# A graph-attention kernel whose last layer multiplies its edge features over 128 rows of the array in place of 30

## What is computed

```python
h = (x @ W.T).reshape(n, H, D)                                # H = 8, D = 32
alpha = einsum('ehd,hd->eh', h[src], a_src) + einsum('ehd,hd->eh', h[dst], a_dst)
enc = relu(edge_attr @ edge_W.T + edge_b).reshape(-1, H, D)   # edge_attr: 53125 x 3
alpha = alpha + sum(enc * h[dst], axis=-1)
alpha = where(alpha >= 0, alpha, 0.2 * alpha)
attn = segment_softmax(alpha, dst)
out = segment_sum(h[src] * attn[..., None], dst) + bias
```

## Time and profile before

| | |
|---|---|
| time, median of 3 runs | 2092.96 us (2092.95 to 2096.61) |
| profiled execution, its own time | 2100.78 us |
| its span, first to last instruction | 2099.0 us |
| mean granted TensorE clock | 0.824 |
| PE busy | 1673.1 us (80%) |
| DVE busy | 1574.9 us (75%) |
| POOL busy | 1504.7 us (72%) |
| ACT busy | 1370.3 us (65%) |

### The profile page before, as it was taken

How to read it: one execution, slowest core, us unless ns; L and a number is a source line. 1 busy time by engine, 2 the same in 40 slices (tenths; PEclk the granted TensorE clock), 3 DMA queues, 4 the chain that set the end, 5 groups by cost and what they waited for, 6 DMA issues and landing times. The chain is left out here.

```text
span 2099.0 us, 43225 instructions
## 1 busy us (share of the span) xinstructions
PE 1673.1 (80%) x9241; PEld 1064.7 (51%) x9241; DVE 1574.9 (75%) x4409; ACT 1370.3 (65%) x5004; POOL 1504.7 (72%) x1648
## 2 busy tenths in 40 slices
PE   7377778777876577878878877789999999999984
PEld 5244445545544344545545444445565655565652
DVE  5567877777778456666656667879899998899997
ACT  3267776777675444545545446668888888888886
POOL 3677777777767577777777773667777777777873
PEclk9578877888787767777777787779999999999995
DMA  7655554555641344444444641434444444444431
GB/s 195 173 161 143 145 143 139 142 144 167 186 116 37 118 129 135 134 129 135 137 129 134 197 121 39 122 109 125 125 129 130 127 130 127 125 128 133 137 90 61
DMA packets 130636, 274.39 MB, mean 131 GB/s; under 512 B 39701, under 2 KB 65274, under 8 KB 130367
## 3 DMA queue, kind: packets, MB, share of 16 engines
q0 software_dynamic: 64128, 181.33, 32.1%
q1 hardware_dynamic: 61564, 86.45, 13.5%
q10 hardware_dynamic: 4699, 3.86, 0.7%
HBM read 255.00 MB, written 17.20 MB: 130 GB/s over the span
## 5 line engine op out<-in xcount | busy, mean ns | idle before, releaser
L1283 POOL DMA_INDIRECT rows<-table,index_all x1100 | 1073.7, 976 | 402.9 <-issue 304.9
L1801 PE MATMUL bank<-rows,onehot 128*128 128x264 f32 (+1 forms) x2200 | 863.2, 492 | 55.0 <-DVE rows L843 17.4
L854 DVE TENSOR_TENSOR sums<-sums,bank 128x264 f32 (+1 forms) x1320 | 556.8, 422 | 325.6 <-PE bank L1801 252.5
L1498 ACT ACTIVATE rows<-rows,wgt 128x33 f32<-128x33 f32 (+2 forms) x2740 | 706.3, 338 | 2.1 <-issue 1.1
L1801 PEld LDWEIGHTS bank<-rows,onehot 128*128 128x128 f32 x2200 | 416.7, 230 | 126.1 <-issue 77.7
L1721 PE MATMUL bank<-identb,onehotT 128*128 128x128 bf16 x1320 | 228.9, 261 | 41.9 <-issue 28.9
L1283 POOL DMA_INDIRECT late<-table,index_all x220 | 214.1, 973 | 67.0 <-issue 62.2
L1721 PEld LDWEIGHTS bank<-identb,onehotT 128*128 128x128 bf16 x1320 | 135.1, 117 | 155.0 <-issue 93.6
L1506 ACT ACTIVATE prod<-bank 128x512 f32<-128x512 f32 x240 | 134.1, 559 | 107.2 <-PE bank L1813 97.0
L1820 PE MATMUL bank<-late,onehotT 128*128 x1320 | 201.0, 290 | 1.3 <-DVE prod L863 1.3
L1450 ACT CAST onehot<-bank 128x768 f32<-128x768 bf16 x240 | 174.5, 729 | 40.5 <-PE bank L1721 40.3
(11 more groups left out here) (215 smaller groups left out, 2242.2 us busy)
## 6 DMA issues: line engine op xcount, KB each, us to landing
locb<-loc_d SPq DMA_DIRECT2D x120, 352.0 KB, 3.8
rows<-table,index_all POOLq DMA_INDIRECT x1100
flags<-flags_d SPq DMA_DIRECT2D x508, 27.5 KB
late<-table,index_all POOLq DMA_INDIRECT x220
table<-rows SPq DMA_DIRECT2D x25, 136.0 KB, 1.8
table<-rows SPq DMA_DIRECT2D x25, 134.0 KB, 2.7
late<-table SPq DMA_DIRECT2D x1, 3300.0 KB
table<-rows SPq DMA_DIRECT2D x25, 129.5 KB, 2.3
```

Source lines behind the costliest of these rows:

```text
L854: done(v.tensor_tensor(a, a, sum_bank(l, t, s)[:, 0:VV], ALU.add), "add")
L1283: g.indirect_dma_start(out=rows_of(l, t)[:, s, 0:ROW[l]], out_offset=None, in_=table[l], in_offset=bass.IndirectOffsetOnAxis(ap=index_all[ ...
L1498: i = a.activation(r, r, ACT.Copy, scale=wgt[:, t.u, h * B + s:h * B + s + 1])
L1801: done(m.matmul(sum_bank(l, t, s)[:, 0:VV], onehot[:, t.u, s, :], rows_of(l, t)[:, s, 0:VV], start=True, stop=True), "agg")
```

## The change

`attrT` is a view of all 128 rows in place of 30, so that the memset of L1264 sets 128 rows to one, and L1813 takes all 128 as its contraction. `edgew3` has 128 rows; a new DVE memset at the start of the program sets them to zero, before the DMAs that write rows 0 to 29. So rows 30 to 127 multiply ones by zeros. Sizes of what is read per row, DMAs and their bytes, and all waits stay.

```diff
-        edgew3 = sb("edgew3", [30, D], BF16)
+        edgew3 = sb("edgew3", [P, D], BF16)
...
-        attrT = lateb[0:30, BLOCKS * 3 * D:].rearrange("p (r f) -> p r f", r=RING)
+        attrT = lateb[:, BLOCKS * 3 * D:].rearrange("p (r f) -> p r f", r=RING)
...
             ones_cols(0)
             mark("ONES_DONE")
+            ch(v.memset(edgew3[:, :], 0.0))
```

## The result

The changed kernel takes 2077.41 us (median of 5 runs, 2071.16 to 2081.35) against 2092.96 us (2090.33 to 2096.61): 0.992 of before, 95% interval 0.9895 to 0.9945. That is faster by 15.6 us where 27.0 were forecast; the time lies inside the range, nearer its upper end. Its profiled execution took 2071.16 us, 29.6 us less than the profiled one of before.

What follows compares the result with a forecast made beforehand. PE was taken to bound low-clock periods, POOL full-clock ones at 16.3 us. From the profiled 2100.78 us, 22.8 (clock) and 3.6 (start) came off: 2074.4 us, or 2066 us on the timed scale, 7.8 us lower; range 2056 to 2082 us.

Steps and rivals of the forecast that it cites:

- The gaps on PE: On PE around each 30-row L1813: going from 128 rows and back costs 0.10 us each way, 0.20 us an encode, removed.
- POOL as the floor of a period: Last layer's full-clock periods: POOL's gathers and four scalings fill 16.3 us, so POOL sets their length.
- full-clock periods gain next to nothing: Last layer's periods at clock 1.00: a faster PE shows next to nothing, since POOL sets them.
- PE is the bound in low periods and gives back 1.2 us in each: Last layer's periods partly at 1.2 GHz: PE saves 0.20 us x 6, so 17.74 us becomes 16.5 us.
- The second case of the rivals: Clock falls as often, only the array's emptying goes: 18 us from the periods, 3.6 us from the start, 2071 us; chance 0.23.
- The clock: the likeliest case: Last layer's 35 periods: the clock stops falling and the low level's 22.8 us come back in full; chance 0.62.
- The start: Last layer's first two periods, bound by PE: 18 encodes x 0.20 us save 3.6 us, between nothing and 7 us.
- The sum: Whole kernel: profiled 2100.78 us less 22.8 and 3.6 gives 2074.4 us, or 2066 us on the timed runs' scale.
- No change: L1813's weight load still waits 0.20 us for the product before it; every period stays, 2093 us; chance 0.08.
- Slower, by more falls: Last layer: PE spends its saving waiting for POOL and DVE, the clock falls twice each period, 2124 us; chance 0.07.
- Memsets at no cost: POOL's L1264 memset takes 3.61 us whatever its rows, far bound 11.8 us more; DVE's 0.1 us falls ahead of an HBM wait.

## Why the prediction came out as it did

**The gaps on PE: right.** 0.60 to 0.50 and 0.32 to 0.22 us, and the weight load beside the sum. The cause needs a correction in size: the gaps stand at 30, 33 and 64 rows, and 65 are enough to avoid them.

**POOL as the floor of a period: wrong.** The sum of POOL's rows came out at 16.3 us, the period's length, and I took the equality for a proof. The earlier trace rows spoke against it: 1.3 us of the idle time that I counted as POOL's own are waits for PE, in five full-clock periods. DVE's 15.5 us looked like room, but its remaining 0.8 us were nothing that a faster PE took away: the full-clock period of the changed kernel has the same 16.30 us with DVE busy for 15.47. Leaving out POOL's work changed nothing; adding 0.39 us to DVE's made the period 0.33 us longer. The forecast that full-clock periods gain next to nothing came true by luck, since another engine sets about the same length. The number was right, the engine was not, and so the advice that follows from it would have been wrong as well: it is DVE's work that is worth moving.

**PE is the bound in low periods and gives back 1.2 us in each: mis-sized.** It measured 0.35 us (17.8 with 64 rows against 17.4 with 65 or 128). The low stretch of a period is short. In one of the kernel before, cut at the ends of its low stretch,

```profile
1553.39:1559.89 6.50, 6.33 (x46) 4.13 (x45) 5.96 (x16) 5.28 (x22) 5.62 (x8) 1.00 0.28 76
1559.89:1563.30 3.41, 3.41 (x14) 2.07 (x13) 3.24 (x9) 2.29 (x10) 2.60 (x3) 0.51 0.46 116
1563.30:1571.15 7.85, 7.15 (x48) 4.45 (x46) 6.69 (x16) 6.76 (x26) 4.93 (x6) 1.00 0.60 174
```

DVE is busy for 3.24 of 3.41 us even there, and the last 7.85 us run at 1.00 again. I read this so: PE's delay holds the period up for a part of it only, and of the six gaps only those in that part count; which ones was not tried apart. The second case of the rivals, put at 18 us from such periods, would have been worth some 15 x 0.35 = 5 us.

**The clock: the likeliest case was right in kind, on no evidence.** The low stretches became few, and that is nearly the whole gain: with 30 or 33 rows four profiles have 12 to 16 low periods and 594.8 to 598.6 us for the 35, mean 596.5; with 128 rows 0 and 7, 575.3 and 582.2 us, mean 578.8. That is 17.7 us where 22.8 were forecast. I had said that no row shows whether rows hold the clock, and took it all the same, so that it came true was luck; 33 rows against 64 shows it.

**The start: right in size, by luck.** Forecast 3.6 us; 44.8 to 41.2 us in the first pair of profiles, 43.6 to 41.1 in the second. POOL's long waits there shrank from the 4.50, 3.64 and 6.07 us of the earlier trace rows to 3.46, 3.44 and 3.71. But the forecast took 18 gaps of 0.20 us for it, and the gaps alone don't give it. The two periods at the start, with 30 rows (second profile), 64 (first), 65 (second) and 128 (first):

```profile
1385.39:1429.01 43.62, 40.04 (x258) 24.04 (x256) 39.44 (x90) 32.05 (x120) 25.05 (x29) 0.91 0.36 96
```

```profile
1387.41:1429.76 42.35, 38.78 (x258) 23.74 (x256) 39.19 (x90) 31.94 (x119) 25.02 (x29) 0.96 0.37 99
```

```profile
1386.94:1429.85 42.91, 37.59 (x257) 26.49 (x255) 38.92 (x89) 31.93 (x120) 25.47 (x29) 0.91 0.36 99
```

```profile
1385.13:1426.37 41.24, 36.11 (x257) 26.06 (x255) 38.83 (x89) 31.81 (x120) 25.13 (x29) 0.99 0.37 102
```

At the same clock of 0.91 the start without gaps (65 rows) is 0.7 us shorter than that with them (30 rows). The rest came with the clock of 0.99, which the sum had not counted there.

**The sum: too large by 11 us, nearly all of it in the clock's term.** It took all falls of one profile as gone, 22.8 us, where 17.7 go in the mean of the profiles. To take off the 7.8 us by which the first profile exceeded the median was fair in the main, since the second, at its median, has as many low periods. The two terms that profiles show, 17.7 and some 3 us, make 20 to 21 us; timed medians show 15.6 and 13.5. Most of the rest lies in which executions were profiled: the two of the changed kernel are 6.3 and 3.0 us faster than the medians of their timed runs, the four with 30 or 33 rows 0.8 us slower in the mean. By these figures the profiles overstate the gain by some 5.5 us, an estimate, and the clock is worth some 12 us in timed runs, about half of the 22.8.

**The rivals.** No change: refuted by the times and by the load that runs beside the sum. Slower, by more falls: refuted, though its first half is what happened: PE does spend its saving waiting for DVE, and the clock holds all the same. **Memsets at no cost: right**, 3.62 us for 128 rows against 3.61 for 30.

## What to carry to other kernels

Where the granted clock dips in a stretch that PE bounds, look for products that use few rows. Here, filling the contraction up with zeros to 64 rows or more cost no PE time (0.12 us from one product to the next with 30 rows, 0.11 with 128) and made the falls of the clock fewer; 33 rows did nothing. Gaps on an engine are worth what the floor leaves of them; find the floor by taking work away from one engine and adding some to another, not from a busy sum that happens to equal the period. Before a gain is read from one profile, count how often its stall comes in other executions.

## What the runs showed of the hardware that I had not expected

The number of rows of a product acts on the granted clock, apart from any gap on PE: 33 rows 13 low periods of 35 and 2095.5 us, 64 rows 6 and 4, and 2082.6 us, with the same instructions and the same gaps of 0.10 us. In all profiles that have low stretches in these periods, they begin at one place, 5.2 to 6.5 us into a period (1559.89 in that of 1553.39 above); PE has then done eleven products of 24 columns (L1735, ended 1.1 to 2.5 us before) and is in or just past those on 1 and 2 rows (L1772, L1781). That these products bring the fall is not shown. The gaps of 0.10 us stand on the way to and from products of 30, 33 and 64 rows, and not of 65.
